# Another order of the steps in the recurrence of a two-layer kernel on one Trainium2 core

## The chip, the cores and the metric

The kernel runs on one core of a Trainium2 chip. A core has TensorE (matrix products, with a queue of weight loads beside them), VectorE, ScalarE, GpSimd (POOL here), and SyncE (SP here), which issues the transfers between HBM and the on-chip SBUF. TensorE writes into PSUM, eight banks of 2 KB per partition; VectorE and ScalarE read and write PSUM too, POOL does not. The engines run their own instruction lists and meet at semaphores.

The metric is the time of one launch on the device in microseconds, as the median of several runs.

## What is computed

Two transformer layers with modulated layer norms on 16 sequences of 512 tokens of width 256. The first layer's mixer is a recurrence over 32 chunks of 16 tokens, for 16 heads of width 16, with two small matrices W_in and W_out (4 x 16 for each sequence and head) as its state:

```python
k_h = softmax(k_t @ W_in.T) * lr[..., 1:];  q_h = softmax(q_t @ W_in.T)
qk = (q_h @ k_h.T) * mask
o_t = q_h @ W_out + qk @ v_t
W_out = W_out + k_h.T @ v_t
for _ in range(2):
    g_out = -attn(W_in, k_t, v_t)       # softmax(W_in k^T / 4) v
    g_in = -attn(W_out, v_t, k_t)
    W_in = W_in - lr_in * g_in
    W_out = W_out - lr_out * g_out
```

A projection with short convolutions comes before the recurrence, and a layer norm, gate and output projection, two feed-forward parts and a windowed attention follow. The change touches none of these.

## The kernel before, in words

The kernel has three phases: the projections (one sequence after another), the recurrence, and everything that follows (two sequences at a time). The recurrence is a hardware loop of 4 rounds of 8 chunks, whose code is written out in full for each of the 8 (`i`, with `c` the number of the chunk). All 16 sequences and 16 heads are done together: 256 pairs lie as 4 tiles `j` of 8 groups times 8 heads. A sum over one head alone is made by a block-diagonal operand. Such an operand is written by `spread`: VectorE does its lower half in one instruction (line 1681, 0.67 us), ScalarE its upper half in four (line 1245, 0.27 us apart). Both halves are needed.

The steps of a chunk have names, and each engine has its own list of them (`re_pe`, `re_act`, `re_dve`, `re_pool`, lines 289 to 298). `mark` counts a semaphore up at each, in the order of the list. `at(c, name)` waits for this chunk's step, `before(c, name)` for that of the chunk before. Nobody reorders anything: each engine does its steps in the order in which they stand.

TensorE (lines 820 to 900), in order: fillers; `a0`, the scores of st_in2 with this chunk's k and q, and `a1`, those of st_in1 with the last chunk's k, in `scores`, line 787; the turns of the raw scores (`traw`, line 837); the turn of e_1 (`te1`, 841); the running sums of tiles 0 and 1 (`sums`, 799); the turn of e_2 (`te2`, 849); the turn of o into columns (`ot`, 814); the state's share of those tiles (`r01`, `add_state`, 807); three updates (`updates`, 794), `p1v` (first inner step of W_out), `p2v` (the last chunk's second step, one chunk late) and `khv` (the product of k_h and v); the turns of w_out_k and w_out_1 (`two`, `tw1`, 868 and 870); `sums(2)`; scores `b0` and `b1` of the two versions of W_out with v (787); `sums(3)`; the turns of their exponentials (`tb0`, `tb1`, 886 and 888); `r23`; the updates `pb0` and `pb1` of W_in (794); the turns of w_in_1 (`ti1`, 897) and w_in_now (`ti`, 900). One scores or updates call is 32 products, each seen in the trace as two passes. Between them stand calls of `keep_busy` (778), products of constants into an unused bank.

ScalarE (1260 to 1308): copies of the raw scores (`rawk`, `rawq`, 1269), the exponentials `e1`, `ek`, `e2` (1271, 1273, 1275), the spreads `x1`, `x2`, `xk`, the copy of k_hat for POOL (`khc`, 1285), o's columns into their block (`oev`, 1251), the copies of two running sums out of PSUM (`evict`, 1263), the spreads `xo` and `xw`, the exponentials `eb0` and `eb1` (1299), the spreads `xb0` and `xb1`, two more copies, and the spreads `xs` and `xi`, on which the next chunk's scores wait.

VectorE (1708 to 1791): maxima and differences for each softmax (1711 to 1722), the sums and scaling of k_hat (`ksum` to `kh`, 1725 to 1734), then for each update a reciprocal, a rate, a product and a sum: `prec` to `pmul` (1741 to 1745), `xrec` to `wo2` (1747 to 1754), `wok` (1757), `wo1` (1759); the scaling of q (`qrec`, `qh`, 1760 and 1764); the spreads; the softmax of b (1772, 1774); and two updates of W_in (1780 to 1786).

POOL takes the copied sums of a tile, weighs them with q_hat and folds them into o (`outputs`, lines 1467, 1472, 1477), and makes the products of k_hat and v for the next sums (`products`, 1504), tiles 0 and 1 first and then 2 and 3. SP loads the next chunk's rows after `p2v` and POOL's last product of the chunk before, loads a block of 64 tokens every fourth chunk after `a1`, and stores a block of o one chunk after that, after `oev`.

## Time and profile before

| | us |
|---|---|
| median of 3 runs (lowest to highest) | 2920.03 (2912.75 to 2925.62) |
| the profiled execution, its own time | 2909.08 |
| its span, first to last instruction | 2907.3 |
| projections, to the recurrence | 0 to 484 |
| recurrence | 484 to 1275 |
| the rest | 1275 to 2907 |

The time is that of a launch; the span is the time between the first and the last instruction of the profiled execution, on the hardware profiler's clock. All other times in this text are from that span's start. In the order of time, neighbouring instructions of one line are merged into one row, with their number behind an x; the number in brackets is the time that the engine stood idle before it, and what released it. "Issue" there means that it waited for nothing that the profile shows. PE is TensorE, PEld its weight loads, DVE is VectorE, ACT is ScalarE.

### The profile page before, as it was taken

To read this page: it belongs to the slowest core of one execution; us is meant where nothing else is said; L and a number is where in the kernel's file an instruction comes from. 1 tells how busy PE (TensorE), PEld (TensorE's weight loads), DVE (VectorE), ACT (ScalarE), POOL (GpSimd) and SP (SyncE) were. 2 spreads that over 40 slices of the span, in tenths; PEclk is the share of its full clock that TensorE was granted. 3 is DMA by queue.
4 is the path that set the end of the run, shared out by engine and by line. 5 is a ranking of instruction groups with operands and counts; after the bars stand their busy time and mean duration, and the time that the engine had idled before them with its cause. 6 is when DMAs were issued, how large, how long until landed. Compare 5 with 4: busy or idle time off the path is not lost.

```text
span 2907.3 us, 90874 instructions
## 1 busy us (share of the span) xinstructions
PE 2504.0 (86%) x33817; PEld 1526.8 (53%) x33817; DVE 1676.1 (58%) x3983; ACT 1620.7 (56%) x4061; POOL 904.5 (31%) x1029
## 2 busy tenths in 40 slices
PE   6999993788787778768999999999999999998998
PEld 4544442555555555533664664655646646546456
DVE  2888873655565556534654655646545545556365
ACT  2887883656565556534644735636536347356354
POOL 0222222545455555541231321321312213213223
PEclk8999996999899999978999999999999999999999
DMA  5555558133313332111111111011011110110110
GB/s 159 147 162 161 161 162 148 27 85 86 69 43 86 71 63 63 42 45 44 44 39 41 25 59 43 17 45 44 16 45 44 60 36 10 59 44 17 45 44 16
DMA packets 386711, 190.06 MB, mean 65 GB/s; under 512 B 271664, under 2 KB 371632, under 8 KB 386224
## 3 DMA queue, kind: packets, MB, share of 16 engines
q1 hardware_dynamic: 386256, 184.01, 24.5%
q8 instruction: 284, 4.65, 0.6%
q14 instruction: 171, 1.40, 0.2%
HBM read 90.10 MB, written 71.30 MB: 56 GB/s over the span
## 4 chain that ended last, share of the span: by engine, by line
PE 55%; issue 16%; DVE 12%; ACT 10%; POOL 5%; DMA 1%; SPq 1%; DVEq 0%; ACTq 0%; POOLq 0%
PE psum L958 9%; PE psum L711 5%; PE psum L799 3%; PE psum L1039 3%; DVE arena L1614 3%; PE psum L1073 3%; PE psum L1062 3%; PE psum L794 3%; PE psum L997 2%; ACT arena L1407 2%; PE psum L787 2%; PE psum L778 2%; ACT arena L1245 2%; PE psum L1091 2%; PE psum L1005 2%
## 5 line engine op out<-in xcount | busy, mean ns | idle before, releaser
L1245 ACT ACTIVATE arena<-psum,scan_sb 64x128 f32<-64x128 f32 x1152 | 310.4, 361 | 139.6 <-PE psum L868 82.0
L1549 POOL TENSOR_TENSOR arena<-arena 128x400 f32<-128x400 f32 x256 | 218.7, 854 | 472.3 <-DVE arena L1942 472.3
L1407 ACT ACTIVATE arena<-psum,arena 128x100 f32<-128x100 f32 x1024 | 268.0, 346 | 127.5 <-DVE arena L1934 127.5
L1934 DVE TENSOR_REDUCE arena<-psum 128x4 f32<-128x400 f32 x256 | 147.1, 575 | 179.3 <-PE psum L1062 177.8
L1467 POOL TENSOR_TENSOR arena<-arena 128x512 f32<-128x512 f32 x132 | 139.8, 1059 | 353.9 <-ACT arena L1263 350.0
L1614 DVE SCALAR_TENSOR_TENSOR arena<-psum,taps_sb,arena 128x511 f32<-128x511 f32 (+2 forms) x288 | 213.6, 747 | 60.7 <-ACT arena L1154 53.9
L711 PE MATMUL psum<-arena,w_in_sb 128*128 128x512 f32 x512 | 229.9, 598 | 0.9 <-issue 0.9
L1681 DVE TENSOR_TENSOR arena<-psum,scan_sb 64x512 f32<-64x512 f32 x290 | 185.9, 673 | 37.8 <-PE psum L886 24.8
L1073 PE MATMUL psum<-ident,arena 128*100 128x128 f32 x1024 | 163.0, 282 | 46.0 <-ACT arena L1413 46.0
L951 PE MATMUL psum<-mask_sb,identb 128*128 128x400 bf16 x960 | 198.9, 342 | 0.0
L778 PE MATMUL psum<-mask_sb,identb 128*128 128x400 bf16 x608 | 163.1, 357 | 35.6 <-issue 32.8
L1445 POOL TENSOR_TENSOR arena<-arena 128x512 f32<-128x512 f32 x64 | 79.6, 1280 | 359.3 <-ACT arena L1180 359.3
L1062 PE MATMUL psum<-arena 64*128 64x100 f32 x2048 | 177.2, 292 | 0.0
L1413 ACT ACTIVATE arena<-psum 100x512 f32<-100x512 f32 x256 | 156.9, 613 | 19.7 <-PE psum L1073 19.7
L794 PE MATMUL psum<-arena 128*32 128x17 f32 x10240 | 121.7, 187 | 48.9 <-issue 48.4
L799 PE MATMUL psum<-arena,scan_sb 128*128 128x512 f32 x264 | 157.5, 705 | 0.8 <-ACT arena L1315 0.8
L1342 ACT ACTIVATE arena<-psum,arena 128x512 f32<-128x512 f32 x96 | 71.7, 772 | 154.3 <-PE psum L969 154.3
L1062 PEld LDWEIGHTS psum<-arena 64*128 64x128 f32 x2048 | 134.1, 186 | 42.1 <-issue 42.1
L711 PEld LDWEIGHTS psum<-arena,w_in_sb 128*128 128x128 f32 x512 | 95.8, 192 | 110.5 <-issue 106.7
L1938 DVE TENSOR_REDUCE arena<-arena 128x4 f32<-128x400 f32 x256 | 143.2, 559 | 4.5 <-ACT arena L1407 4.5
L1073 PEld LDWEIGHTS psum<-ident,arena 128*100 128x100 f32 x1024 | 102.9, 128 | 81.2 <-ACT arena L1413 68.2
L794 PEld LDWEIGHTS psum<-arena 128*32 128x32 f32 x10240 | 107.6, 112 | 71.8 <-issue 60.4
(219 smaller groups left out, 5036.8 us busy)
## 6 DMA issues: line engine op xcount, KB each, us to landing
arena<-arena SPq DMA_DIRECT2D x144, 128.0 KB
arena<-x SPq DMA_DIRECT2D x32, 512.0 KB, 4.1
arena<-o_d SPq DMA_DIRECT2D x18, 512.0 KB, 5.9
arena<-gate_d SPq DMA_DIRECT2D x18, 512.0 KB, 6.7
v_rows_d<-arena SPq DMA_DIRECT2D x64, 136.0 KB
k_rows_d<-arena SPq DMA_DIRECT2D x64, 136.0 KB
arena<-k_rows_d SPq DMA_DIRECT2D x128, 68.0 KB, 2.1
arena<-v_rows_d SPq DMA_DIRECT2D x128, 68.0 KB, 2.2
```

Source lines behind the costliest of these rows:

```text
L711: mm = pe.matmul(bank[2 + j % 6][:], w_in_sb[:, k, j * P:(j + 1) * P], a_h[:, k], start=(k == 0), stop=(k == KT - 1))
L778: pe.matmul(bank[5][:, 0:2 * KT * KEYS], identb[:], mask_sb[:, 0:2].rearrange("p a b -> p (a b)"), start=True, stop=True)
L794: mm = pe.matmul(dst[j * NST:(j + 1) * NST, x], by_tile(pb)[:, j, x], rows[:, j * PP + x], start=True, stop=True)
L799: return pe.matmul(bank[6 + j % 2][:], causal, kv[:, j], start=True, stop=False, skip_group_check=True)
L951: pe.matmul(spare[:, 0:2 * KT * KEYS], identb[:], mask_sb[:, 0:2].rearrange("p a b -> p (a b)"), start=True, stop=True)
L958: mm = pe.matmul(B(s, banks[a])[:, j * DIM:(j + 1) * DIM], lhs(k, 2 * a + j), rhs(k), start=(k == 0), stop=(k == KT - 1))
L1062: mm = pe.matmul(B(s, top)[:, k * KEYS:(k + 1) * KEYS], c_qb[s][rows, k, f], c_k[s][rows, k, f], start=False, stop=True, skip_group_check= ...
L1073: mm = pe.transpose(bank[TURNED][0:KEYS, tok(u)], c_soft[s][:, f % 2, u], ident[:])
L1245: ins = act.activation(dst.rearrange("p (t x a) -> p t x a", x=PP, a=INNER)[upper, :, x], src.rearrange("p (t a) -> p t a", a=INNER)[upper ...
L1407: act.activation(c_soft[s][:, f % 2, u], sc, ACT.Exp, bias=c_max[s][:, u:u + 1]).then_inc(c_act.mark(f"exp{s}{f}u{u}"), 1)
L1549: pool.tensor_tensor(soft, soft, c_rec[s].unsqueeze(2).broadcast_to([P, 4, KEYS]), ALU.mult).then_inc(c_pool.mark(f"prob{s}{f}"), 1)
L1614: ins = dve.scalar_tensor_tensor(out=a_acc[:, t, j:TOK], in0=bank[2 + t][:, 0:TOK - j], scalar=taps_sb[:, t % KT, col:col + 1], in1=a_acc[ ...
```

## The change

The steps of a chunk are the same, with the same operands, in another order on three engines:

- TensorE: `a1` before `a0`; `te2` right behind `a0`; `p2v` between `sums(0)` and `sums(1)`; then `r01`, `khv`, `p1v` where it was `r01`, `p1v`, `p2v`, `khv`; `ot` behind `tw1`; `sums(2)` behind `b1`, `sums(3)` behind `tb1`; `r23` behind `pb1`. The chunk has 9 fillers where it had 19.
- ScalarE: `e2` first, `x2` between `e1` and `ek`; `oev` behind `xb1`; the copies of tiles 2 and 3 behind `xi`, so at the end of the chunk.
- VectorE: `xmax` and `xsub` first, `x2` before `ksum`; `xrec` to `wok` before `prec` to `wo1`; `qrec` and `qh` behind `bs1`.
- `b1` and its turn use bank 0 in place of bank 1. The wait of `xk` for the last chunk's `khv` goes; `ksub` gets one for the last chunk's `ek`.

The new lists show the order, and the cut of TensorE's code what moves:

```diff
         re_dve = Steps(sem("re_dve"), [
-            "amax", "asub", "kmax", "xmax", "ksub", "xsub", "ksum", "krec", "x1", "krl", "kh", "x2", "xk",
-            "prec", "plr", "pmul", "xrec", "xlr", "xmul", "wo2", "wok", "wo1", "qrec", "qh", "xo", "xw",
-            "bm0", "bs0", "bm1", "bs1", "xb0", "xb1", "irec0", "ilr0", "imul0", "wi1", "irec1", "ilr1", "imul1", "wi", "xs", "xi"])
+            "xmax", "xsub", "amax", "asub", "kmax", "ksub", "x2", "ksum", "krec", "x1", "krl", "kh", "xk",
+            "xrec", "xlr", "xmul", "wo2", "wok", "prec", "plr", "pmul", "wo1", "xo", "xw",
+            "bm0", "bs0", "bm1", "bs1", "qrec", "qh", "xb0", "xb1", "irec0", "ilr0", "imul0", "wi1", "irec1", "ilr1", "imul1", "wi", "xs", "xi"])
...
-        re_act = Steps(sem("re_act"), ["rawk", "rawq", "e1", "ek", "e2", "x1", "x2", "xk", "khc", "oev", "rv0", "rv1", "xo", "xw",
-                                       "eb0", "eb1", "xb0", "xb1", "rv2", "rv3", "xs", "xi"])
-        re_pe = Steps(sem("re_pe"), ["a0", "a1", "traw", "te1", "te2", "ot", "r01", "p1v", "p2v", "khv", "two", "tw1", "b0", "b1",
-                                     "tb0", "tb1", "r23", "pb0", "pb1", "ti1", "ti"])
+        re_act = Steps(sem("re_act"), ["e2", "rawk", "rawq", "e1", "x2", "ek", "x1", "xk", "khc", "rv0", "rv1", "xo", "xw",
+                                       "eb0", "eb1", "xb0", "xb1", "oev", "xs", "xi", "rv2", "rv3"])
+        re_pe = Steps(sem("re_pe"), ["a1", "a0", "te2", "traw", "te1", "p2v", "r01", "khv", "p1v", "two", "tw1", "ot", "b0", "b1",
+                                     "tb0", "tb1", "pb0", "pb1", "r23", "ti1", "ti"])
...
-                    keep_busy(4)
+                    keep_busy(2)
+                    pe.wait_ge(dve.sem, dve.before(c, "xs"))
+                    pe.wait_ge(act.sem, act.before(c, "xs"))
+                    scores(grid(bank[2][:, 3 * P:4 * P], CHUNK), st_in1, kq_blk[past][:, :, :, 0, then], every).then_inc(mine.mark("a1"), 1)
+                    keep_busy(1)
...
-                    scores(grid(bank[2][:, 3 * P:4 * P], CHUNK), st_in1, kq_blk[past][:, :, :, 0, then], every).then_inc(mine.mark("a1"), 1)
+                    pe.wait_ge(act.sem, act.at(c, "e2"))
+                    pe.transpose(bank[2][:, 2 * P:3 * P], e_2, ident[:]).then_inc(mine.mark("te2"), 1)
                     keep_busy(1)
...
-                    keep_busy(3)
                     pe.wait_ge(dve.sem, dve.at(c, "wok"))
                     pe.transpose(bank[3][:, 3 * P:4 * P], w_out_k, ident[:]).then_inc(mine.mark("two"), 1)
+                    keep_busy(2)
                     pe.wait_ge(dve.sem, dve.at(c, "wo1"))
                     pe.transpose(bank[0][:, 2 * P:3 * P], w_out_1, ident[:]).then_inc(mine.mark("tw1"), 1)
...
-                    add_state((2, 3), before_last).then_inc(mine.mark("r23"), 1)
-                    keep_busy(2)
                     for r, b in enumerate((3, 0)):
...
-                    keep_busy(3)
+                    add_state((2, 3), before_last).then_inc(mine.mark("r23"), 1)
                     pe.wait_ge(dve.sem, dve.at(c, "wi1"))
                     pe.transpose(bank[2][:, 0:P], w_in_1, ident[:]).then_inc(mine.mark("ti1"), 1)
-                    keep_busy(3)
+                    keep_busy(2)
```

On ScalarE:

```diff
+                    act.wait_ge(dve.sem, dve.at(c, "xsub"))
+                    act.activation(e_2, e_2, ACT.Exp, scale=attn).then_inc(mine.mark("e2"), 1)
                     act.wait_ge(pe.sem, pe.at(c, "a0"))
...
-                    evict(2)
-                    evict(3)
+                    act.wait_ge(pe.sem, pe.at(c, "ot"))
...
+                    out_cols(past // CPB, past % CPB).then_inc(mine.mark("oev"), 1)
                     act.wait_ge(pe.sem, pe.at(c, "ti1"))
                     spread(st_in1, bank[2][:, 0:P]).then_inc(mine.mark("xs"), 1)
                     act.wait_ge(pe.sem, pe.at(c, "ti"))
                     spread(st_in2, bank[1][:, 0:P]).then_inc(mine.mark("xi"), 1)
+                    evict(2)
+                    evict(3)
```

## Rows read from the trace of the kernel before

**Rows 1.** The page: busy time, granted clock in 40 slices, queue of instructions.

```profile
PE 2504.0 (86%) x33817; PEld 1526.8 (53%) x33817; DVE 1676.1 (58%) x3983; ACT 1620.7 (56%) x4061; POOL 904.5 (31%) x1029
...
PEclk8999996999899999978999999999999999999999
...
q8 instruction: 284, 4.65, 0.6%
```

**Rows 2.** Busy time by stage: from:to, length, engines, PEclk, DMA share, GB/s.

```profile
484.00:1275.00 791.00, 637.81 (x20677) 416.63 (x20676) 459.11 (x1342) 470.39 (x1574) 420.30 (x517) 0.93 0.29 63
```

**Rows 3.** Line L900, the last transpose: duration min/median/max, first and last start.

```profile
L900 PE MATMUL psum<-ident,arena x32: 273/328/329, 507.2 to 1262.3; 128*128 128x128 f32 x32
```

**Rows 4.** Groups of TensorE, 484 to 1275 us: busy, mean | idle before, releaser.

```profile
L794 PE MATMUL psum<-arena 128*32 128x17 f32 x10240 | 121.7, 187 | 48.9 <-issue 48.4
L787 PE MATMUL psum<-arena 128*32 128x16 f32 x8064 | 95.8, 192 | 45.6 <-issue 25.4 <-ACT arena L1245 17.9 <-DVE arena L1681 0.9
```

**Rows 5.** Order of time in one chunk: start, length, engine, line, idle before.

```profile
632.24 1.21 PEld L787 LDWEIGHTS psum<-arena 128*32 128x32 f32 x128 [0.98 <-ACT arena L1245]
...
633.05 0.45 ACT L1269 ACTIVATE arena<-psum 128x128 f32<-128x128 f32 x2 [0.85 <-PE psum L787]
...
635.13 0.39 ACT L1273 ACTIVATE psum<-arena 128x256 f32<-128x256 f32 x1 [0.56 <-DVE arena L1719]
...
637.07 0.30 DVE L1734 TENSOR_TENSOR psum<-psum,arena 128x128 f32<-128x128 f32 x1
...
638.41 1.70 PE L794 MATMUL psum<-arena 128*32 128x17 f32 x138
...
641.30 0.64 PE L794 MATMUL psum<-arena 128*32 128x17 f32 x54 [1.19 <-issue]
```

**Rows 6.** The same view, the second half of the chunk.

```profile
640.01 0.21 DVE L1747 RECIPROCAL psum<-psum 128x8 f32<-128x8 f32 x1
...
642.00 0.29 DVE L1757 TENSOR_TENSOR arena<-arena,psum 128x128 f32<-128x128 f32 x1 [0.84 <-PE psum L794]
...
642.85 1.12 PE L799 MATMUL psum<-arena,scan_sb 128*128 128x512 f32 x2
...
643.31 1.27 DVE L1681 TENSOR_TENSOR arena<-psum,scan_sb 64x512 f32<-64x512 f32 x2
...
644.10 0.64 PEld L787 LDWEIGHTS psum<-arena 128*32 128x32 f32 x64 [0.62 <-ACT arena L1245]
...
645.33 0.64 PEld L787 LDWEIGHTS psum<-arena 128*32 128x32 f32 x64 [0.59 <-ACT arena L1245]
...
647.45 2.15 ACT L1245 ACTIVATE arena<-psum,scan_sb 64x128 f32<-64x128 f32 x8 [0.36 <-PE psum L886]
...
649.62 1.09 ACT L1263 ACTIVATE arena<-psum 128x512 f32<-128x512 f32 x2
...
650.30 1.06 POOL L1467 TENSOR_TENSOR arena<-arena 128x512 f32<-128x512 f32 x1 [2.92 <-ACT arena L1263]
...
651.37 2.15 ACT L1245 ACTIVATE arena<-psum,scan_sb 64x128 f32<-64x128 f32 x8 [0.66 <-PE psum L897]
...
653.57 1.21 PEld L787 LDWEIGHTS psum<-arena 128*32 128x32 f32 x128 [0.98 <-ACT arena L1245]
...
655.01 2.23 POOL L1504 TENSOR_TENSOR arena<-arena 128x512 f32<-128x512 f32 x2
```

**Rows 7.** The same view, two later rounds at the same place of the code.

```profile
691.79 0.38 PE L794 MATMUL psum<-arena 128*32 128x17 f32 x21 [3.16 <-issue]
...
890.60 0.51 PE L794 MATMUL psum<-arena 128*32 128x17 f32 x21 [2.89 <-issue]
```

**Rows 8.** The same view, TensorE in the round's fourth chunk.

```profile
553.16 1.31 PE L787 MATMUL psum<-arena 128*32 128x32 f32 x128 [0.58 <-ACT arena L1245]
556.83 0.49 PE L778 MATMUL psum<-mask_sb,identb 128*128 128x400 bf16 x1 [2.36 <-issue]
```

**Rows 9.** Busy time of a stretch, columns as in rows 2.

```profile
692.80:696.00 3.20, 3.20 (x50) 1.44 (x52) 1.76 (x5) 2.15 (x8) 2.66 (x4) 0.50 1.05 228
```

More of the change, by code:

```diff
@@ L845, in _ @@
                     sums(0)
+                    pe.wait_ge(dve.sem, dve.at(c, "x2"))
+                    pe.wait_ge(act.sem, act.at(c, "x2"))
+                    updates(grid(bank[2][:, 0:PP * ROW17], ROW17), pb_2, v_rows[(i - 1) % 2], every).then_inc(mine.mark("p2v"), 1)
                     pe.wait_ge(pool.sem, pool.before(c, "kv1"))
                     sums(1)
-                    pe.wait_ge(act.sem, act.at(c, "e2"))
-                    pe.transpose(bank[2][:, 2 * P:3 * P], e_2, ident[:]).then_inc(mine.mark("te2"), 1)
+                    add_state((0, 1), before_last).then_inc(mine.mark("r01"), 1)
+                    pe.wait_ge(rows_loaded[i % 2], 16 * 2 * JJ * (n * (CPR // 2) + i // 2 + 1))
+                    pe.wait_ge(dve.sem, dve.at(c, "xk"))
+                    pe.wait_ge(act.sem, act.at(c, "xk"))
+                    updates(grid(bank[3][:, 0:PP * ROW17], ROW17), pb_kh, v_rows[i % 2], every).then_inc(mine.mark("khv"), 1)
+                    pe.wait_ge(dve.sem, dve.at(c, "x1"))
+                    pe.wait_ge(act.sem, act.at(c, "x1"))
+                    updates(grid(bank[0][:, 0:PP * ROW17], ROW17), pb_1, v_rows[i % 2], every).then_inc(mine.mark("p1v"), 1)
+                    pe.wait_ge(dve.sem, dve.at(c, "wok"))
+                    pe.transpose(bank[3][:, 3 * P:4 * P], w_out_k, ident[:]).then_inc(mine.mark("two"), 1)
+                    keep_busy(2)
+                    pe.wait_ge(dve.sem, dve.at(c, "wo1"))
+                    pe.transpose(bank[0][:, 2 * P:3 * P], w_out_1, ident[:]).then_inc(mine.mark("tw1"), 1)
                     pe.wait_ge(pool.sem, pool.before(c, "sb3"))
@@ L879, in _ @@
                     pe.wait_ge(act.sem, act.at(c, "xw"))
-                    scores(grid(bank[1][:, 2 * P:3 * P], CHUNK), st_out2, v_blk[buf][:, :, :, now], every).then_inc(mine.mark("b1"), 1)
+                    scores(grid(bank[0][:, 2 * P:3 * P], CHUNK), st_out2, v_blk[buf][:, :, :, now], every).then_inc(mine.mark("b1"), 1)
+                    pe.wait_ge(act.sem, act.at(c, "rv0"))
+                    pe.wait_ge(pool.sem, pool.before(c, "kv2"))
+                    sums(2)
+                    pe.wait_ge(act.sem, act.at(c, "eb0"))
+                    pe.transpose(bank[2][:, 3 * P:4 * P], e_b[:, 0], ident[:]).then_inc(mine.mark("tb0"), 1)
+                    pe.wait_ge(act.sem, act.at(c, "eb1"))
+                    pe.transpose(bank[0][:, 3 * P:4 * P], e_b[:, 1], ident[:]).then_inc(mine.mark("tb1"), 1)
                     pe.wait_ge(act.sem, act.at(c, "rv1"))
@@ L883, in _ @@
                     sums(3)
-                    keep_busy(1)
-                    pe.wait_ge(act.sem, act.at(c, "eb0"))
-                    pe.transpose(bank[2][:, 3 * P:4 * P], e_b[:, 0], ident[:]).then_inc(mine.mark("tb0"), 1)
-                    pe.wait_ge(act.sem, act.at(c, "eb1"))
-                    pe.transpose(bank[1][:, 3 * P:4 * P], e_b[:, 1], ident[:]).then_inc(mine.mark("tb1"), 1)
-                    add_state((2, 3), before_last).then_inc(mine.mark("r23"), 1)
-                    keep_busy(2)
                     for r, b in enumerate((3, 0)):
@@ L1708, in _ @@
                     c = n * CPR + i
+                    dve.wait_ge(pe.sem, pe.at(c, "a1"))
+                    dve.tensor_reduce(m_x, x_now, AX.X, ALU.max).then_inc(mine.mark("xmax"), 1)
+                    dve.wait_ge(mine.sem, mine.at(c, "xmax"))
+                    dve.wait_ge(pe.sem, pe.before(c, "te2"))
+                    dve.tensor_tensor(eights(e_2, CHUNK), x_now, over(m_x, CHUNK), ALU.subtract).then_inc(mine.mark("xsub"), 1)
                     dve.wait_ge(act.sem, act.at(c, "rawk"))
```

75 lines of the change are left out of this document (24 added, 51 removed).

## The prediction

> **What bounds the kernel now.** I read the page first: TensorE is busy 86% of the span, but that share mixes stages [rows 1]. The busy time by stage puts the recurrence, the only code the change touches, at 484 to 1275 us, and there no engine is full: TensorE 638 of 791 us, ScalarE 470, VectorE 459, POOL 420 [rows 2]. The last transpose of a chunk comes 32 times, first at 507.2 and last at 1262.3 us, so a chunk takes 755.1/31 = 24.4 us on average [rows 3]. It is a loop of dependences over four engines, in which each chunk's first scores wait for the spreads that end the chunk before.
>
> So the view to read is the order of time in one undisturbed chunk, from the scores of st_in2 at 632.24 us to the same scores at 653.57 us: 21.33 us. I give times as offsets from 632.24. The first half is held by TensorE, which goes without a break from e_1's transpose over two running sums, o's turn, the state term and the updates [rows 5]. Then something no semaphore explains: the updates' 192 passes break off after 138 and go on at 641.30, after 1.19 us of "issue" [rows 5]. In two successive rounds of the loop 21 passes are left over at the same place of the code, behind waits of 3.16 and 2.89 us [rows 7]. A wait tied to a place of the code and released by no engine looks like instructions arriving late: the page has a queue of kind "instruction" that brought 4.65 MB in 284 packets, 16.4 KB each [rows 1]. Over the stage such waits are 48.4 us in front of update passes and 25.4 in front of scores [rows 4]. They follow the densest code, where two passes of 32 columns take 10 ns each to load. The second half is a relay: w_out_k and w_out_1, their turns, spreads, scores b0 and b1, exponentials, turns, spreads, updates, turns, spreads [rows 6].
>
> **The change, part by part, as a walk of one chunk.** Durations are those of rows 5 and 6; hand-overs of 0.03 to 0.06 us as there.
>
> *Start.* a1's scores (64 passes, 0.65 us) are issued before a0 and need only the earlier spread, so they fit while ScalarE still spreads st_in2. They leave a0's shadow at no cost: cover is the 1.08 us of four spreads; without it they would cost 0.65. But the two last copies of run (1.09 us a pair) now stand on ScalarE right behind the last spread, and e_2's exponential (0.3) too, ahead of the copies of the raw scores. Those copies ended at 1.26 in the old chunk; now 1.04 + 0.03 + 0.3 + 0.03 + 0.45 = 1.85. **Cost 0.6 us.** xmax and xsub (0.3 each) run before that and hide behind the copies of run.
>
> *Up to the k-path.* kmax was at 1.91, now 2.49; without xmax between, ksub ends at 3.35. e_1's exponential ends at 2.65, and now x2's four spreads (1.08) stand ahead of ek: ek ends at 4.18, against 3.28. From there to the end of kh were 1.85 us (637.37 against 635.52), so kh ends at 6.03 and ScalarE's spread of it at 7.14. **kh's updates can start at 7.2**; their first 10 passes (138 less 128) went near 7.75 before, ahead of the wait.
>
> *TensorE beside it.* te1 to 3.0, a running sum (0.9) to 3.9, p2v to 4.55, the other sum to 5.45, the state term (1.1) to 6.55. o's turn (0.6) is gone from here. TensorE stands 0.65 us before kh's updates. They and p1v are now a run of 128 passes after a pause, not 192 after dense work, so **the wait of 1.19 us should go**: kh's updates end at 7.85 against 9.70.
>
> *W_out.* xrec to wo2 run beside this (1.15 us from 6.75) and end at 7.9, just in time. wok ends at 8.25. But p1v ends only at 8.5, and prec, plr, pmul, wo1 (another 1.15) end at 9.75; st_out1's spread stands behind them on VectorE and ends at 10.42. So b0 starts at 10.5 against 11.86: **1.35 gained**, less than the 1.85 of the line above, since the chain of p1v is now in the open (old way 1.44 from updates to spread, now about 2.1). b1 and its turn move from bank 1 to bank 0, which only makes b1 wait for a spread it waits for anyway. q's scaling (0.34 and 0.29) is gone from in front of it, to behind bs1, where VectorE waits for a turn anyway. o's turn (0.6) lies between w_out_1's turn and b0, beside that spread. ScalarE needs the k_hat copy and two evictions in front of the spread: the copy waits for POOL's last product. POOL began on tiles 2 and 3 at 650.30 and ended at 657.24, 6.9 us later [rows 6]; its source is copied at 0.5 now, so it ends near 7.6. Copy and evictions end at 9.0 and the spread at 10.1, hidden by 0.3 us.
>
> *Queues.* SP's loads of the next rows wait for p2v and POOL's last product, so they go at about 7.6 (7.8 before); p2v comes 2 us sooner and decides nothing. The eviction of o (0.59) moves from the middle of ScalarE's queue to behind the spreads of pb (15.35 to 15.95), where ScalarE waits 1.5 us for the turn of w_in_1; without that cover it would cost its 0.59. The store of a block that waits for it goes some 8 us later, one chunk in four, and its buffer is wanted again only chunks later: nothing.
>
> *b0 to the spreads of pb.* b1 no longer sits behind a late instruction (0.31) and starts at 11.25. The running sum is behind b1 and before the turn of e_b (ends 12.8); the second exponential ends at 13.05, the turn at 13.4, the spreads start at 13.2. Old: 15.21 against b0 at 11.86, 3.35 apart; now 2.7. **0.65 gained.**
>
> *Tail.* Spreads to pb1's start 2.15 as before, 15.4, end 16.05. The state term for tiles 2 and 3 (1.1 us, dense) stood before pb0 with two fillers, beside the spreads. Now it stands between pb1 and the turn of w_in_1, which was ready at about 0.6 us: turn at 17.15, spreads 17.5. From spreads to spreads that is 4.3, was 3.92. **Cost 0.38.** Two spreads (2.15) to 19.65, a0 at 19.7.
>
> Sum for this chunk: 0.6 lost at the start lies inside the first 10.5, so -1.35 - 0.65 + 0.38 = -1.6 us, 21.33 to 19.7. Over 32 chunks that is -51 us. Ten fewer fillers a chunk, 0.17 us of TensorE each, are already in these sums where they stood on the path; elsewhere they are nothing.
>
> **What no row shows.** Where late instructions fall in the new code. Bounds: none on the path (0), or the same 1.2 us once a chunk (+38 us in all). The other runs of 64 to 128 passes (a1 with a0, b0 with b1, pb0, pb1 and the state term) have pauses in or before them; nearest is the chunk's b0, which lost 0.31. I take 0.4 us, +13 us. On the other side, a0 and a1 in one run were followed by a wait of 2.36 us in the fourth chunk of the round [rows 8], and one like it stands in the fifth; parted, I take 2 us off one chunk in four, -16 us (ends 0 and -19). The transfers of a block, issued after a1, start about 1 us sooner in a chunk and still collide with instruction packets; I count them at nothing (+10 to -20 us). The wait at the loop's start and the table load stay. Sum -51 + 13 - 16 = -54, rounded to -50.
>
> The Trainium skill (Runtime: NRT & Kernel Launch, Instruction fetch mechanics) says instructions come in 16 KiB blocks and that crossing one is mostly hidden. The packet size agrees with the page of this profile; the waits of rows 5 and 7 do not look hidden. If that rule held, they would be something else and stay, which is the first rival.
>
> The profiled execution took 2909.08 us, of which 2907.3 are its span; the median of three is 2920.03. 2909 - 50 = 2859; against the median it is 2870. A measurement of this kernel can tell about 0.5% (15 us) from no change.
>
> **Rivals.**
>
> *The waits do not go.* They are tied to places of the code, and a new order only has new places: perhaps 1.2 us in a chunk at p1v, and 0.3 at b1. For it: the old chunks nearly all have one. Against: it comes after 138 dense passes, and no new run has more than 128. Then -1.6 + 1.5 = -0.1 us a chunk, with the rest nothing: about 2915. Chance 0.18.
>
> *The clock of TensorE falls* (slower). The granted clock was 0.93 in this stage, so it is at its lower level 14% of the time [rows 2]; it was 0.50 (1.2 instead of 2.4 GHz) from 692.8 to 696.0, after the wait of 3.16 us, and a pair of passes of a running sum took 1.98 us there against 1.12 [rows 6, 9]. From 17.5 to 2.4 of the next chunk the new order has only small scores, turns and 7 fillers where there were 12, and pauses of 0.3 and 0.7 us. If the lower level holds from the turn of e_2 to the second state term, four running sums cost 0.86 each and the turns some 0.15 each, with 0.65 of slack at kh: about +3 us a chunk, 1.4 more than the gain, 2920 + 45 = 2965. It decides once the lower level covers more than half of a chunk. Against: pauses before falls were 1.2 us and up, mine are shorter. Chance 0.12.
>
> The Trainium skill (TensorE: Matmul & The Clock Gate, HAM oscillation) warns that an engine idling between bursts runs each burst at half rate. The trace agrees for the long waits; by that rule removed fillers speak against this change, which is this rival.
>
> *Forecast*: gain as walked, chance 0.70, own range 2830 to 2905: at the one end 2 us a chunk, the fourth and fifth chunks and the transfers (-90), at the other the evictions and late instructions eating all but 0.5 a chunk (-16).
>
> **How the numbers follow.** Predicted 2870. The range leaves out most of the clock case (0.12) and some 0.08 at the fast end: 2830 to 2925. The case of waits that stay lies within 0.5%; the slow case is slower. Chances 0.70, 0.18, 0.12.
>
> **What would show it.** Right: chunks near 19.7 to 20.3 us; no "issue" of 1 us inside the updates; issue in front of updates well under 48 us in the stage; the copies of the raw scores 0.6 us later behind the scores; b0 some 10.5 us after a0. Wrong: a granted clock well under 0.93 in the stage; "issue" at p1v, b1 or the state term; ScalarE ending the wait for b0 (POOL's product later than 7.6); or chunks at 21 us or more without such waits, which would mean that a hand-over of the walk is missing.

## The result, and the profile after

The changed kernel is slower by 1%: its median is 2950.94 us (2940.84 to 2962.38, 7 runs) beside 2921.98 (2912.75 to 2932.51, 7 runs) for the kernel before, a ratio of 1.0104 with an interval of 1.0083 to 1.0124. The profiled execution's span is 2949.1 us where it was 2907.3. (By the medians the kernel lost 29 us, by the two profiled executions 42: the profiled one of the kernel before, 2909.08 us, was faster than any of its seven.)

The page of the changed kernel, the lines that answer to [rows 1]:

```profile
PE 2516.5 (85%) x33497; PEld 1522.8 (52%) x33497; DVE 1689.9 (57%) x3983; ACT 1632.0 (55%) x4061; POOL 901.2 (31%) x1029
...
PEclk8999996988989989869999999989999999999999
...
q8 instruction: 283, 4.64, 0.7%
```

320 passes of TensorE are gone (ten fillers in each of 32 chunks), and the granted clock has more slices below 9. To see in which part of the kernel the time went, split the span at the recurrence's end. Busy time by stage of the changed kernel, columns as in [rows 2]:

```profile
484.00:1266.00 782.00, 613.51 (x20339) 395.23 (x20339) 470.51 (x1340) 481.84 (x1571) 415.16 (x513) 0.90 0.29 64
1266.00:2949.00 1683.00, 1509.51 (x11623) 911.36 (x11621) 884.90 (x2040) 826.18 (x1945) 400.09 (x438) 0.95 0.14 38
```

and the kernel before, its last phase:

```profile
1275.00:2907.00 1632.00, 1474.02 (x11604) 894.34 (x11604) 883.10 (x2040) 826.45 (x1944) 398.15 (x434) 0.97 0.14 39
```

The last transpose of a chunk, the changed kernel:

```profile
L899 PE MATMUL psum<-ident,arena x32: 271/273/421, 505.4 to 1250.7; 128*128 128x128 f32 x32
```

From the first last-transpose to the 32nd are 745.3 us where [rows 3] had 755.1. So the recurrence did get shorter, by 9.8 us, and starts 1.8 us sooner. From there to the end of the span are 2949.1 - 1250.7 = 1698.4 us, before 2907.3 - 1262.3 = 1645.0. **The loss of 53.4 us lies in code that the change does not touch.** The three parts make 53.4 - 9.8 - 1.8 = 41.8, the difference of the spans.

The last phase is a loop of 8 passes over two sequences each. Its first products, before and after (duration min/median/max, first and last start, then the idle time before them and before their weight loads together, in us and times), kernel before:

```profile
L944 PE MATMUL psum<-gates_row,arena x64: 587/587/1212, 1320.1 to 2708.2; 16*128 16x512 f32 x64
...
  issue: 16.0, 55
```

changed kernel:

```profile
L943 PE MATMUL psum<-gates_row,arena x64: 798/1056/1216, 1309.9 to 2750.5; 16*128 16x512 f32 x64
...
  issue: 64.3, 60
```

Between the first and the last of them lie 1388.1 us before and 1440.6 after: 52.5 us in seven returns of the loop, 7.5 a return. The order of time at one return, kernel before:

```profile
1710.50 7.07 PE L958 MATMUL psum<-arena 128*128 128x256 f32 x32
1717.50 4.67 PE L944 MATMUL psum<-gates_row,arena 16*128 16x512 f32 x8
```

changed kernel:

```profile
1710.49 7.07 PE L957 MATMUL psum<-arena 128*128 128x256 f32 x32
...
1720.70 5.92 PE L943 MATMUL psum<-gates_row,arena 16*128 16x512 f32 x7 [3.15 <-issue]
```

The last products of a pass run straight into the first of the next before; after the change TensorE waits 3.15 us there, for nothing that the profile shows, and then needs 0.85 us a product (5.92/7) where it needed 0.58 (4.67/8). The median product went from 587 to 1056 ns. That is the lower level of the clock: granted were 0.54 from 1720.7 to 1727.0 us after the change; before it, 1.00 from 1717.5 to 1720.1 and then 0.50 too, though there TensorE had not waited. So the clock falls near this place in both kernels, and with the wait it falls sooner after the first product and stays low longer. The waits at the seven returns (3.0 to 3.4 us each) make 22 of the 52.5 us; the rest goes with the clock, whose mean from the first to the last of these products was 0.98 before and 0.95 after. The wait looks like those of [rows 5] and [rows 7], at a new place, seven times over.

Inside the recurrence, groups of TensorE in the changed kernel, columns as in [rows 4]:

```profile
L794 PE MATMUL psum<-arena 128*32 128x17 f32 x10240 | 125.8, 189 | 36.2 <-issue 20.7 <-ACT arena L1244 10.5 <-DVE psum L1779 3.4
L787 PE MATMUL psum<-arena 128*32 128x16 f32 (+1 forms) x8064 | 106.2, 193 | 48.4 <-issue 38.8 <-ACT arena L1244 7.4 <-DVE arena L1766 0.4
L778 PE MATMUL psum<-mask_sb,identb 128*128 128x400 bf16 x284 | 87.6, 368 | 15.0 <-issue 15.0
L807 PE MATMUL psum<-arena,scan_sb 32*128 32x128 f32 x1040 | 78.7, 291 | 7.9 <-issue 7.9
```

"Issue" ahead of updates fell from 48.4 to 20.7 us, as foretold. Ahead of scores it rose from 25.4 to 38.8, and ahead of the state term from 0.8 to 7.9. These waits repeat at the same instruction of each round. The order of time in two successive rounds of the changed kernel:

```profile
617.59 1.16 PE L807 MATMUL psum<-arena,scan_sb 32*128 32x128 f32 x16 [1.81 <-issue]
...
637.94 0.25 PE L787 MATMUL psum<-arena 128*32 128x16 f32 x7 [1.72 <-issue]
...
812.71 1.65 PE L807 MATMUL psum<-arena,scan_sb 32*128 32x128 f32 x16 [1.84 <-issue]
...
833.45 0.25 PE L787 MATMUL psum<-arena 128*32 128x16 f32 x7 [1.84 <-issue]
```

Behind the first of these waits the granted clock is 0.50 from 619 to 622 us, behind that of 812.71 from 815 to 818 and by then already lower within the 16 passes (1.65 us for 1.16).

Mean time of each of the eight chunks of a round in the two kernels, from the distances between last transposes (us; the first of a round holds the loop's return):

| | 1 | 2 | 3 | 4 | 5 | 6 | 7 | 8 |
|---|---|---|---|---|---|---|---|---|
| before | 30.7 | 21.5 | 22.5 | 24.7 | 29.8 | 24.1 | 21.7 | 21.4 |
| after | 31.1 | 21.9 | 20.9 | 21.1 | 24.1 | 24.8 | 27.3 | 23.0 |

The fourth and fifth chunk gained 3.6 and 5.7 us, the seventh and eighth lost 5.6 and 1.6.

Now an undisturbed chunk, the scores of st_in2 at 918.35 to the same at 939.12: 20.77 us. Order of time, changed kernel, the rows to be held against the walk:

```profile
918.35 0.76 PE L787 MATMUL psum<-arena 128*32 128x32 f32 x64
...
919.65 0.42 ACT L1270 ACTIVATE arena<-psum 128x128 f32<-128x128 f32 x2
...
920.14 0.72 POOL L1470 TENSOR_TENSOR arena<-arena 128x256 f32<-128x256 f32 x1
...
920.26 0.75 DVE L1717 TENSOR_TENSOR arena<-arena 128x128 f32<-128x128 f32 x1
...
921.04 0.31 ACT L1272 ACTIVATE arena<-arena 128x128 f32<-128x128 f32 x1 [0.97 <-DVE arena L1717]
...
924.47 0.30 DVE L1735 TENSOR_TENSOR psum<-psum,arena 128x128 f32<-128x128 f32 x1
...
925.98 1.41 PE L794 MATMUL psum<-arena 128*32 128x17 f32 x128 [0.46 <-ACT arena L1244]
...
926.77 0.29 DVE L1750 TENSOR_TENSOR arena<-arena,psum 128x128 f32<-128x128 f32 x1 [0.22 <-PE psum L794]
926.80 1.06 POOL L1465 TENSOR_TENSOR arena<-arena 128x512 f32<-128x512 f32 x1 [1.00 <-ACT arena L1262]
...
927.45 0.22 DVE L1752 RECIPROCAL psum<-psum 128x8 f32<-128x8 f32 x1 [0.39 <-PE psum L794]
...
927.84 0.17 DVE L1754 TENSOR_TENSOR arena<-psum,arena 128x8 f32<-128x8 f32 x1 [0.18 <-DVE psum L1752]
...
928.33 0.30 DVE L1756 TENSOR_TENSOR psum<-psum,arena 128x128 f32<-128x128 f32 x1 [0.32 <-DVE arena L1754]
928.66 0.29 DVE L1758 TENSOR_TENSOR arena<-arena,psum 128x128 f32<-128x128 f32 x1
...
929.77 0.74 PE L787 MATMUL psum<-arena 128*32 128x16 f32 x64
...
930.67 0.73 PE L787 MATMUL psum<-arena 128*32 128x16 f32 x64 [0.16 <-ACT arena L1244]
...
932.60 2.14 ACT L1244 ACTIVATE arena<-psum,scan_sb 64x128 f32<-64x128 f32 x8 [0.20 <-PE psum L884]
...
936.92 2.14 ACT L1244 ACTIVATE arena<-psum,scan_sb 64x128 f32<-64x128 f32 x8 [1.55 <-PE psum L896]
```

The 128 passes at 925.98 run through without a break: the 1.19 us of "issue" of [rows 5] is gone. The chunk gained 0.6 us where the walk had 1.6.

### The profile page after: what moved, and what is told of

Read it like the earlier page. It is cut to its first block, busy times and chain, and to the rows that moved or that the text cites. A ratio compares the mean times of both kernels' runs of the same rounds, so it can differ in the third digit from the quotient of the medians.

```text
span 2949.1 us, 90330 instructions
## 1 busy us (share of the span) xinstructions
PE 2516.5 (85%) x33497; PEld 1522.8 (52%) x33497; DVE 1689.9 (57%) x3983; ACT 1632.0 (55%) x4061; POOL 901.2 (31%) x1029
## 3 DMA queue, kind: packets, MB, share of 16 engines
q1 hardware_dynamic: 386256, 184.01, 23.9%
## 4 chain that ended last, share of the span: by engine, by line
PE 55%; issue 14%; DVE 14%; ACT 12%; POOL 2%; DMA 1%; SPq 1%; DVEq 1%; ACTq 0%; POOLq 0%
PE psum L957 9%; PE psum L711 5%; PE psum L794 3%; ACT arena L1244 3%; PE psum L1038 3%; PE psum L799 3%; DVE arena L1612 3%; PE psum L1061 3%; PE psum L1072 3%; PE psum L996 2%; PE psum L787 2%; ACT arena L1405 2%; PE psum L943 2%; PE psum L950 2%; PE psum L1004 2%
## 5 line engine op out<-in xcount | busy, mean ns | idle before, releaser
L1244 ACT ACTIVATE arena<-psum,scan_sb 64x128 f32<-64x128 f32 x1152 | 317.6, 357 | 154.7 <-PE psum L896 74.0
L950 PE MATMUL psum<-mask_sb,identb 128*128 128x400 bf16 x960 | 203.6, 348 | 0.0
L799 PE MATMUL psum<-arena,scan_sb 128*128 128x512 f32 x264 | 172.9, 743 | 0.9 <-ACT arena L1313 0.8
L794 PE MATMUL psum<-arena 128*32 128x17 f32 x10240 | 125.8, 189 | 36.2 <-issue 20.7
L787 PE MATMUL psum<-arena 128*32 128x16 f32 x8192 | 108.3, 194 | 48.4 <-issue 38.8
```

The source lines that it names most:

```text
L794: mm = pe.matmul(dst[j * NST:(j + 1) * NST, x], by_tile(pb)[:, j, x], rows[:, j * PP + x], start=True, stop=True)
L799: return pe.matmul(bank[6 + j % 2][:], causal, kv[:, j], start=True, stop=False, skip_group_check=True)
L950: pe.matmul(spare[:, 0:2 * KT * KEYS], identb[:], mask_sb[:, 0:2].rearrange("p a b -> p (a b)"), start=True, stop=True)
L1244: ins = act.activation(dst.rearrange("p (t x a) -> p t x a", x=PP, a=INNER)[upper, :, x], src.rearrange("p (t a) -> p t a", a=INNER)[upper ...
```

## The experiments

My theory of the loss: the change made TensorE's instruction list inside the recurrence 144 instructions shorter (160 fewer for the 80 fillers of a round, which are a weight load and a pass each, 16 more for waits), which moves everything behind it, and with it the head of the last loop, against the blocks in which instructions are fetched. The rival: a real effect of the new order, carried over into the last phase. Counted in the compiled lists in blocks of 256 instructions, the head of the last loop stands at 46.62 before and at 46.06 after. The size of a block is an assumption, which e2 tests; the counts themselves no trace shows, only their differences. Padding is made of tiny products of constants into an unused bank, two instructions each, run once. The numbers "stage" and "rest" below are the time between first and 32nd last transpose and from there to the span's end, taken as above (before: 755.1 and 1645.0; after: 745.3 and 1698.4). Experiments of one group ran on one chip and share their runs of the kernel before, with medians of 2908.94, 2908.32 and 2918.41 us; each group had another chip. A ratio is safe from that. A stage of one group beside a stage of another, or beside those of the result, is not wholly, and each is read from one profiled execution.

### Group 1: the place of the last loop

**e1: the change with 144 instructions of padding behind the recurrence.** The head of the last loop is back at .62 of a block.

```diff
+            for _ in range(72):
+                pe.matmul(bank[5][:, 0:8], identb[:], mask_sb[:, 0, 0:8], start=True, stop=True)
```

> The changed kernel with 72 tiny products (144 instructions, counting a weight load and a pass each) on TensorE between the recurrence and the last phase, where TensorE stands idle 12 us anyway. They put the last phase's loop as far into the list of instructions as it was before the change. Theory 'placement': the last phase, which the change does not touch, got 53 us longer only because its loop moved 144 instructions forward and now breaks across blocks of instructions at its start; so the issue wait of 3.15 us at each of the loop's returns goes, a pass through the loop takes 198 us again instead of 205, and the kernel ends near 2950 - 54 = 2896, some 0.8% faster than before. Rival 'clock': the phase is slower because of what precedes it in time (fewer fillers, another phase of the clock's steps): the loop stays at 205 us and the kernel at 2950.

2896.54 us (2885.76 to 2915.54, 12 runs), ratio 0.9964 (0.9941 to 0.9986); stage 731.6, rest 1652.1. The first products of the last phase, e1:

```profile
L945 PE MATMUL psum<-gates_row,arena x64: 587/587/1210, 1298.3 to 2690.2; 16*128 16x512 f32 x64
```

1391.9 us for the seven returns, 48.7 less than in the changed kernel: of the 53.4 us lost in the rest, 46.3 went with the place. That the stage also fell, 745.3 to 731.6, was not to be expected, since all of its instructions stand where they stood; the padding is behind it. No run explains it. A plain candidate lies in the measuring: the kernel before took 2921.98 us beside the result and 2908.94 in this group, 13 us less with nothing changed at all, and the stage fell by 14. The changed kernel was not run again here, so this stays open. The profiled execution of the kernel before, 2909.08 us, is at this group's level too; part of what the stage of the two kernels compares (755.1 and 745.3) may therefore be this difference.

**e2: the kernel before with 112 instructions of padding**, which put its last loop where the change put it (47.06).

```diff
+            for _ in range(56):
+                pe.matmul(bank[5][:, 0:8], identb[:], mask_sb[:, 0, 0:8], start=True, stop=True)
```

> The kernel before, with 56 tiny products (112 instructions) at the same place. 112 forward is the same as 144 back if instructions come in blocks of 256 (16.4 KB by the page, 64 bytes each), so the last phase's loop lies in its blocks as in the changed kernel, while the recurrence is that of before. Placement: the loop's passes take 205 us with a wait of about 3 us at each return, and the kernel is near 2921 + 54 = 2975. Clock: no change, 2921.

2951.15 us (2950.39 to 2955.56, 5 runs), ratio 1.0146 (1.0123 to 1.0168); stage 761.2, rest 1685.4. The last products of a pass and the first of the next, e2:

```profile
1720.10 7.07 PE L960 MATMUL psum<-arena 128*128 128x256 f32 x32
1730.36 5.48 PE L946 MATMUL psum<-gates_row,arena 16*128 16x512 f32 x6 [3.19 <-issue]
```

The old order, with nothing changed but 56 products that run once, has the same wait, and loses 40.4 us in the rest. Expected were 54 us more than the kernel before; by the medians it is 42. And 112 instructions forward do what 144 back did: the two places differ by 256 instructions, as they should if a block has 256.

**e3: the change with 16 instructions of padding** (8 products in place of 72; head at 46.12).

> The changed kernel with 8 tiny products (16 instructions). If it is the loop's first few instructions that lie at the end of one block, so that two blocks have to be fetched one after the other at each return, 16 are enough to push them into the next block and the result is that of the 144, near 2896. If the whole length of the shift matters (how much of the last block is left to run when the loop returns), it stays near 2950.

2899.12 us (12 runs), ratio 0.9981 (0.9957 to 1.0004); stage 729.1, rest 1652.3. First products, e3:

```profile
L945 PE MATMUL psum<-gates_row,arena x64: 587/690/1211, 1296.5 to 2688.8; 16*128 16x512 f32 x64
```

1392.3 us as in e1. Sixteen instructions more are enough, so it is no matter of total length: at .06 of a block by my count the loop's head is dear, at .12 or .62 it is not. Why, the runs do not say. The expectation took the loop's first instructions to lie at the end of a block, while my count puts the head 15 instructions behind a block's start; the count could be off by a few instructions, and nothing here settles which picture is right.

**e4: the change with the 19 fillers of before**, and 240 instructions of padding, 120 products, left out below (head at .62).

```diff
-                    keep_busy(2)
+                    keep_busy(4)
...
-                    keep_busy(1)
+                    keep_busy(2)
...
+                    keep_busy(2)
```

> The changed order with the 19 fillers a chunk of before (4, 2, 2, 2, 4, 2, 3), and 240 instructions of padding, which put the last phase's loop where it was before. It tells apart what the removed fillers did inside the recurrence, which became 10 us shorter where 50 were expected. If too few fillers cost it the clock (granted 0.89 in this stage against 0.93), the stage gets shorter than in the kernel with 144: 10 to 20 us. If the losses are late instructions beside transfers and the order's own waits, more fillers gain nothing and cost what of them lies on the path, 0 to 15 us.

2886.05 us (2874.6 to 2903.19, 9 runs), ratio 0.9923 (0.9898 to 0.9947); stage 727.7, rest 1653.4. Busy time of the recurrence, e1 and then e4:

```profile
484.00:1254.00 770.00, 606.70 (x20356) 392.87 (x20355) 470.20 (x1339) 481.81 (x1569) 417.82 (x516) 0.90 0.28 64
```

```profile
484.00:1251.00 767.00, 640.69 (x20662) 416.90 (x20662) 469.92 (x1339) 480.70 (x1568) 417.36 (x516) 0.93 0.28 65
```

The granted clock is back at 0.93 and the stage is some 4 us shorter although TensorE has 34 us more to do. By the medians of all runs e4 is 10.5 us faster than e1 (the intervals of the two ratios just overlap). So the fillers that were removed were worth keeping, but less in the stage than the 10 to 20 us that were expected. How much of the 4 us is clock and how much that the late instructions fall elsewhere, the run does not tell: its fifth chunk takes 28.3 us (e1: 23.0) and its seventh 20.7 (27.1).

### Group 2: the place of the recurrence, and the order of two updates

**e5 and e6: both orders with their recurrence 96 instructions later**, and the last loop at .62 in both. In e5 (the change) 48 products stand ahead of the recurrence and 24 behind, in e6 (the old order) 48 and 80.

```diff
+            for _ in range(48):
+                pe.matmul(bank[5][:, 0:8], identb[:], mask_sb[:, 0, 0:8], start=True, stop=True)
```

> The changed kernel with 96 instructions of padding ahead of the recurrence's loop and 48 behind it, so that the last phase's loop lies as before the change and only the recurrence's own code is moved, by 96 instructions, against the blocks it is fetched in. If the shortfall inside the recurrence (some 25 us gained of the 50 forecast) comes from late instructions at places of the code, the slow chunks of a round (the seventh at 27 us beside 20.6 for an undisturbed one) become other chunks, each undisturbed chunk stays at 20.6, and the recurrence moves by up to 15 us either way. If it comes from the order itself or from transfers that belong to a chunk, the seventh stays slow.

> The kernel before with the same shift of its recurrence (96 ahead, 160 behind, a whole block of 256 in all). It says how much of any comparison of the two orders is luck with the blocks: its update waits should sit at other places, undisturbed chunks stay at 21.4 us since its run of 192 passes holds a boundary wherever it lies, and the whole stays within 0.5% of before. If the old order's 1.2 us of waiting went away with the shift, its chunks would fall to 20.2.

e5: 2910.24 us (11 runs), ratio 1.0011 (0.9991 to 1.0031), stage 754.3, rest 1651.0. e6: 2933.86 us (5 runs), 1.0081 (1.0056 to 1.0107), stage 785.1, rest 1640.5. The last transposes, e5 and then e6:

```profile
L901 PE MATMUL psum<-ident,arena x32: 272/273/421, 501.7 to 1256.0; 128*128 128x128 f32 x32
```

```profile
L902 PE MATMUL psum<-ident,arena x32: 273/328/421, 506.5 to 1291.6; 128*128 128x128 f32 x32
```

Moving the recurrence alone costs 754.3 - 731.6 = 22.7 us with the new order and 785.1 - 755.1 = 30.0 with the old. What one profiled execution says of a place must be read with a margin, though: with the head unmoved, the old order took 755.1 and 761.2 us (before, e2) and the new one 745.3, 731.6 and 729.1 (after, e1, e3). The means are 758.2 and 735.3, so the new order wins 22.8 us there (10 to 32 by pairs) and 30.8 at the other place, 0.7 to 1.0 us a chunk. The place is worth as much as the order. The ratios say the same of the place: e5 1.0011 beside e1 0.9964, e6 1.0081 beside 1. Inside the loop the two orders still have their late instructions at different steps; what stands here is the sum.

The expectation of e5 held in kind and missed in size: the slow chunks became other ones (the third to fifth, 26.1, 27.6 and 30.0 us) and the undisturbed ones stayed at 20.6 and 20.7, but the recurrence moved by more than 15 us. That of e6 missed: no chunk stayed at 21.4 us, the shortest takes 22.9, and the kernel left the 0.5% that it was given.

**e7: e1 with `p1v` ahead of `khv` on TensorE, and `prec`, `plr` ahead of `wok` on VectorE**, to take p1v's chain back out of the open.

```diff
-            "xrec", "xlr", "xmul", "wo2", "wok", "prec", "plr", "pmul", "wo1", "xo", "xw",
+            "xrec", "xlr", "xmul", "wo2", "prec", "plr", "wok", "pmul", "wo1", "xo", "xw",
...
-        re_pe = Steps(sem("re_pe"), ["a1", "a0", "te2", "traw", "te1", "p2v", "r01", "khv", "p1v", "two", "tw1", "ot", "b0", "b1",
+        re_pe = Steps(sem("re_pe"), ["a1", "a0", "te2", "traw", "te1", "p2v", "r01", "p1v", "khv", "two", "tw1", "ot", "b0", "b1",
```

> The changed kernel with 144 instructions of padding, and p1v ahead of khv on TensorE, with prec and plr ahead of wok on VectorE. In the changed kernel w_out_1's chain waits for p1v, which stands behind khv though its operand is ready 2 us sooner, while TensorE stands idle 0.65 us in front of khv. My walk of a chunk left this chain open at 2.1 us and it measured 2.9. If that step was mis-sized as I think, b0 starts 0.7 to 0.9 us sooner in each chunk: undisturbed chunks near 19.9 us, the kernel 20 to 25 us under the one with padding alone (2896), so near 2874. If something else sets b0 (ScalarE's copies behind POOL), nothing or a loss.

2895.47 us, ratio 0.9948 (0.993 to 0.9967); stage 738.2, rest 1649.6. Order of time in one chunk, e7:

```profile
549.26 0.76 PE L787 MATMUL psum<-arena 128*32 128x32 f32 x64
...
560.03 0.60 PE L787 MATMUL psum<-arena 128*32 128x16 f32 x48 [0.18 <-ACT arena L1246]
561.38 0.80 PE L787 MATMUL psum<-arena 128*32 128x16 f32 x58 [0.74 <-issue]
```

b0 comes 10.77 us after a0, not 11.42: the exchange does what it was to do. But b0 itself now breaks off after 48 passes for 0.74 us (the view ends at 562 us, within the last row), and the gain is gone in this chunk; the third chunk of a round fell from 20.8 to 20.2 us, the second rose from 20.6 to 22.3. Over the stage it lost 6.6 us, which is within the margin, and the ratio's interval overlaps that of e1: nothing gained that can be told, where 20 to 25 us were expected.

**e8: e4 with the same exchange.**

> The same exchange in the kernel with 19 fillers (2886). With the fillers' 10 us and the exchange's 22 adding up it is near 2864, 1.5% faster than before. If the added fillers then stand on the path (two of them between the turns of w_out_k and w_out_1), it gains less than the kernel with 9.

2885.61 us (9 runs), ratio 0.9925 (0.99 to 0.9951); stage 729.0. The same as e4, and not the 2864 us that were expected. Beside e7, on the same chip, the fillers bring 9.9 us by the medians and 9.2 in the stage.

### Group 3: POOL beside VectorE, and more places

**e9: e1 with POOL's weighing of the running sums and its first fold cut from 512 elements a partition to 16 and from 256 to 32.** It leaves out nearly all of the weighing with q_hat and most of the first fold, so its time is that of a lighter POOL.

```diff
-                return pool.tensor_tensor(terms(run[:, j]), terms(run[:, j]), by_a, ALU.mult)
+                return pool.tensor_tensor(terms(run[:, j])[:, 0:1, 0:1], terms(run[:, j])[:, 0:1, 0:1], by_a[:, 0:1, 0:1], ALU.mult)
...
-                return pool.tensor_tensor(t[:, :, 0:2], t[:, :, 0:2], t[:, :, 2:4], ALU.add)
+                return pool.tensor_tensor(t[:, 0:1, 0:2], t[:, 0:1, 0:2], t[:, 0:1, 2:4], ALU.add)
```

> The changed kernel with 144 instructions of padding, in which POOL weighs and folds only a single pair of a tile (it leaves out the weighing of the running sums by q_hat and their first fold, so the output o is not computed; the products of k_hat and v stay). In the changed order the difference for e_1 (L1717) took 0.75 us beside POOL's weighing, against 0.29 elsewhere, and the chain prec to wo1 1.5 us against the 1.15 of my walk. If VectorE is held up by POOL's work on the same memory, the 0.75 becomes 0.29 and undisturbed chunks fall from 20.6 to some 19.9 us, the kernel by 15 to 25 us from 2896. If the 0.75 comes from something else, chunks stay at 20.6 and only the end of the recurrence gets shorter, by some 10 us.

2899.53 us (11 runs), ratio 0.9949 (0.9923 to 0.9975); stage 736.5. The difference for e_1 (duration min/median/max), e1 and then e9:

```profile
L1719 DVE TENSOR_TENSOR arena<-arena x32: 291/743/1156, 482.9 to 1220.4; 128x128 f32<-128x128 f32 x32
```

```profile
L1719 DVE TENSOR_TENSOR arena<-arena x32: 291/294/1146, 483.1 to 1222.2; 128x128 f32<-128x128 f32 x32
L1714 DVE TENSOR_TENSOR arena<-psum,arena x32: 290/291/295, 481.2 to 1220.5; 128x128 f32<-128x128 f32 x32
```

With most of POOL's work out of the way the instruction takes 0.29 us; beside it 0.74. The same subtraction for e_2, which reads one side from PSUM, is 0.29 each time, but in e1 POOL stands idle beside 25 of its 32. A fairer comparison is the sum wok, which also reads one side from PSUM: POOL works beside it in every chunk of the changed kernel (926.77 above), and it takes 0.29 us. Chunks 2 to 4 of a round fell from 20.6, 20.8 and 21.0 to 20.0, 20.3 and 20.5 us: this contention is worth 0.5 us of an undisturbed chunk, not the 0.7 expected. The stage did not follow (731.6 to 736.5), the last two chunks of the round took it back (27.1 and 21.9 to 27.9 and 23.9), and the 15 to 25 us expected of the kernel did not come: the two ratios are alike.

**e10, e11 and e12: e8 with the recurrence 160, 224 and 64 instructions later**, the last loop kept at .62 (80, 112 and 32 products ahead, 40, 8 and 88 behind).

> The kernel with 19 fillers and p1v first (2886), with 160 instructions of padding ahead of the recurrence and the last phase's loop kept in its place. If places of the code decide, the recurrence, 729 us at no shift, is moved by up to 30 us either way and the slow chunks are other ones; with 32 or more places open to it I expect the sum between 725 and 755, so the kernel between 2882 and 2912. If places only matter for the orders tried so far, it stays within 5 us.

> The same with 224 ahead. The same expectation; it is one of three more places that say how wide the spread is, and whether the place of the kernel as handed in was a good or a bad one.

> The same with 64 ahead. The changed kernel with 96 lost 23 us against none, the kernel before 30 us. If that came from the distance of the loop's own start to a block's boundary and not from the places inside its chunks, 64 lies between 0 and 96 and gives about two thirds of that loss, near 2900; if the places inside count, nothing ties it to those two.

e10: 2925.68 us, ratio 1.0019 (1.0 to 1.0038), stage 765.9. e11: 2899.3 (6 runs), 0.9919 (0.9885 to 0.9953), stage 734.4. e12: 2912.06, 0.9999 (0.9975 to 1.0023), stage 753.1. The recurrence of one and the same order takes 729.0, 753.1, 765.9 and 734.4 us at shifts of 0, 64, 160 and 224 instructions. That is 37 us, or 1.3% of the kernel, though the first was read on another chip; by the ratios, which are safe from that, the place alone moves the kernel by 1.0% (0.9919 to 1.0019). The expectation had 725 to 755 us for e10 and e11, and e10 lies outside it. For e12 it named a rival, that only the distance of the loop's own start from a block's boundary counts, with about two thirds of the loss at 96 instructions: the stage lost 24.1 us at 64, as much as e5 lost at 96 with another order, and e11 lost 5.4 at 224. That speaks against the rival but does not exclude it. e4, e8 and e11, at 0.992 of the time of before, are the best versions found.

## Why the prediction was wrong

Predicted was 2870 us (2830 to 2925), with 0.12 for slower; measured 2951. Against the profiled execution the sum was to be -50; it is +41.8: 53.4 lost behind the recurrence, 11.6 gained up to its end.

**The step that failed is one that was never written as a step: that everything outside the recurrence keeps its time.** The prediction asks where late instructions fall in the new code, and bounds them by 0 and 38 us, inside the recurrence only. It had the mechanism (places in the code, 16.4 KB packets, [rows 1, 5, 7]) but took the shorter list of TensorE for nothing outside the chunk. The 144 instructions fewer moved the last loop's head to a place in its block where its return is dear, and the seven returns cost 52.5 us in all. e2 shows this with the old order, e3 mends it with 16 instructions. The Trainium skill (Runtime: NRT & Kernel Launch, Instruction fetch mechanics) says that a taken branch whose target lies outside the two blocks held forces a fetch and a stall. A round of the last loop is some 1450 passes of TensorE (11604/8), each with a weight load, so by the count above its head is outside in both kernels. The trace shows the stall of 3.15 us after and none before, so by the runs the head's place in its block decides, which that rule does not say.

**The rivals.** The slow one was another mechanism: the clock of TensorE in a chunk. It fell from 0.93 to 0.90 in the stage, but in the rows shown it fell behind new waits of 1.8 us (617.59 and 812.71), not from the shorter pauses that this rival feared: the undisturbed chunk, which has those, was granted 1.00 throughout, and its 64 passes take 0.74 us. It is the smaller part: with the fillers of before the stage is 4 us shorter in e4 and 9 in e8, net of where their longer code puts late instructions. "The waits do not go" was half right. The waits at updates went (48.4 to 20.7), and over scores, updates, fillers and state term "issue" fell from 107.4 (with 32.8 in front of fillers and 0.8 at the state term) to 82.4 us, but new ones came where the text named them as signs, at the state term (1.81) and b1 (1.72).

**The terms of the walk**, against the chunk from 918.35:

- Copies of the raw scores: foretold to end at 1.85, they end at 1.72. Right.
- e_1's exponential: 2.65 foretold, 3.00 measured. The difference asub was taken as 0.29 us and takes 0.75 beside POOL's fold at 920.14. Even in the undisturbed chunk of before it had taken 0.55, beside POOL's products; over all chunks its median went from 396 to 744 ns. e9 shows the cause. kh ends at 6.42 (6.03) and the updates start at 7.63 (7.2). **0.4 us too little.**
- khv and p1v without a break: right, the 1.19 us is gone. But they ended at 9.04, not 8.5: **0.1 more**.
- p1v's chain from prec to wo1: 1.15 taken, 1.50 measured, 927.45 to 928.95. **0.35 too little.** 0.18 us of waiting for its own reciprocal was left out. The wait of 0.32 in front of L1756 is one of four chunks alone, as that line's own view says (us, times):

```profile
  DVE arena L1754: 1.3, 4
```

- b0 at 11.42 (10.5) and b1 at 12.32 (11.25), then spreads at 14.25 (13.2). From b0 to the spreads 2.83 (2.7): right but for 0.1.
- The tail, from spreads to spreads 4.32 (4.3) and to a0 another 2.20 (2.2). Right: moving the state term behind pb1 costs what was said.

So the undisturbed chunk gave -0.6 for -1.6, and at equal place of the recurrence 0.7 to 1.0 a chunk over the whole stage, 23 to 31 us in place of 51. The two kernels of the result, one execution each, show 9.8.

**The fourth and fifth chunk**: foretold -16 us; they gained 3.6 and 5.7 us each in 4 rounds, 37 us, but the seventh and eighth gave back 29. **Late instructions** (+13 us taken) were the largest uncertainty in the stage: by e5, e6 and e10 to e12 the place of the code moves the stage by 5 to 37 us.

## What to carry to other kernels

An edit that changes how many instructions an engine has also moves all the code behind it, and on TensorE here that cost more than the edit gave: run it once more with a few harmless instructions ahead of the next loop before judging it. Look first at the untouched phases of the profile, and at the first instruction after each loop's return. When an instruction of VectorE that reads only SBUF is moved, look at what POOL does beside it.

## What the runs showed of the hardware that was not expected

- 16 instructions on TensorE, run once, moved the kernel's ratio to the one before from 1.0104 to 0.9981: at a loop's return 3.15 us of "issue", followed by products of 1056 ns in place of 587.
- The recurrence took 745.3 us in the changed kernel and 731.6 and 729.1 in e1 and e3, whose TensorE code up to its end is the same. These are one execution each, and the kernel before was 13 us slower by its median beside the first than beside the others; no run tells whether the padding behind it has a part in it.
- The same code in the same place does not always have the same last phase: in the profiled execution of e11 a pass of the last loop takes 201.0 us on average, in those of e1, e10 and e12 198.3 or 198.4. Its runs spread from 2882.21 to 2919.09.
- A subtraction of VectorE with both inputs in SBUF takes 0.74 us (median) beside POOL's weighing and folding and 0.29 with them cut down; an instruction of the same size with one input in PSUM takes 0.29 beside POOL. The Trainium skill (GPSIMD Engine Reference, Specifications) names contention for VectorE instructions with two SBUF inputs; e9 agrees.
